# RWKV, quantised FFN and attention on one core: layernorm roots moved to a seed and a cubic, two operations moved to GpSimd, and new instruction orders

## What is computed

```python
def wkv(time_decay, time_first, k, v):
    w, u = -jnp.exp(time_decay), time_first
    def step(carry, kv):
        aa, bb, pp = carry
        ww = u + kk
        qq = jnp.maximum(pp, ww)
        e1, e2 = jnp.exp(pp - qq), jnp.exp(ww - qq)
        out = (e1 * aa + e2 * vv) / (e1 * bb + e2)
        qq2 = jnp.maximum(pp + w, kk)
        ...
for l in range(L):                        # 4 layers
    h = layernorm(x, ln1_w[l], ln1_b[l]); hh = time_shift(h)
    k, v, sr = ...                        # three products of mixes of h and hh
    x = x + (sr * wkv(...)) @ Wo[l].T
    h = layernorm(x, ln2_w[l], ln2_b[l]); hh = time_shift(h)
    x = x + sigmoid(xr @ Wcr[l].T) * (square(relu(xk @ Wck[l].T)) @ Wcv[l].T)
```

## Time and profile before

| | |
|---|---|
| time, median of 3 runs | 1373.0 us (1369.5 to 1373.78) |
| profiled execution, span on the core | 1368.5 us |
| the profiled execution's own time | no other than the span is recorded for it; the runs lie 1.0 to 5.3 us above the span |
| TensorE busy | 1303.0 us, 95% |
| VectorE busy | 1238.3 us, 90% |
| ScalarE busy | 1257.6 us, 92% |
| GpSimd busy | 1122.6 us, 82% |

### The profile page before, as it was taken

How to read it: one execution, slowest core, us unless ns; L and a number is a source line. 1 busy time by engine, 2 the same in 40 slices (tenths; PEclk the granted TensorE clock), 3 DMA queues, 4 the chain that set the end, 5 groups by cost and what they waited for, 6 DMA issues and landing times.

```text
span 1368.5 us, 23485 instructions
## 1 busy us (share of the span) xinstructions
PE 1303.0 (95%) x7285; PEld 935.9 (68%) x7285; DVE 1238.3 (90%) x2169; ACT 1257.6 (92%) x2539; POOL 1122.6 (82%) x1216
## 2 busy tenths in 40 slices
PE   3799999999999999999999999988999998899997
PEld 1356677667766677667766677766777876677776
DVE  6999999999999999999999999569999577978994
ACT  6899999999999999999999999877887899998884
POOL 6888998888888888888899999979998465666784
PEclk9899999999999999999999999999999999999999
DMA  7000000000000000000000000010000000000011
GB/s 237 1 1 1 1 1 1 1 21 13 1 0 2 1 1 1 1 1 1 1 1 1 8 24 21 27 32 1 1 1 1 2 1 1 1 16 16 24 32 39
DMA packets 26923, 18.54 MB, mean 14 GB/s; under 512 B 1072, under 2 KB 26160, under 8 KB 26800
## 3 DMA queue, kind: packets, MB, share of 16 engines
q1 hardware_dynamic: 26800, 17.05, 4.2%
HBM read 12.85 MB, written 4.19 MB: 12 GB/s over the span
## 4 chain that ended last, share of the span: by engine, by line
PE 67%; ACT 11%; DVE 9%; POOL 6%; issue 5%; DMA 0%; SPq 0%; DVEq 0%; ACTq 0%; POOLq 0%
PE ps L1154 12%; PE ps L1137 12%; PE ps L1213 5%; PE ps L1037 4%; PE ps L1192 4%; PE ps L1185 4%; PE ps L1144 3%; PE ps L1124 3%; PE ps L1089 3%; PE ps L1090 3%; PE ps L1102 3%; PE ps L1082 3%; PE ps L1263 3%; PE ps L1201 2%; PE ps L1245 2%
## 5 line engine op out<-in xcount | busy, mean ns | idle before, releaser
L1137 PE MATMUL ps<-xk,W 128*128 128x512 f32 x512 | 250.7, 593 | 1.4 <-ACT kf L864 1.4
L1154 PE MATMUL ps<-W,kf 128*128 128x128 f32 x2048 | 249.6, 275 | 0.0
L754 ACT ACTIVATE z<-X,ln_rs 128x128 f32<-128x128 f32 x512 | 239.7, 720 | 3.7 <-POOL ln_rs L603 3.7
L1154 PEld LDWEIGHTS ps<-W,kf 128*128 128x128 f32 x2048 | 239.2, 192 | 2.3 <-issue 1.0
L864 ACT ACTIVATE kf<-ps 128x512 f32<-128x512 f32 x256 | 186.6, 817 | 0.5 <-PE ps L1137 0.5
L871 ACT ACTIVATE kf<-kf 128x1024 f32<-128x1024 f32 x128 | 164.6, 1286 | 0.0
L1037 PEld LDWEIGHTS ps<-idn,z 128*128 128x128 f32 x664 | 83.1, 143 | 113.3 <-issue 87.3
L1137 PEld LDWEIGHTS ps<-xk,W 128*128 128x128 f32 x512 | 91.9, 190 | 92.1 <-issue 89.0
L710 POOL TENSOR_TENSOR W<-W,hsc 128x704 f32<-128x704 f32 x64 | 88.8, 1388 | 59.0 <-DVE W L493 58.8
L1037 PE MATMUL ps<-idn,z 128*128 128x128 f32 x664 | 102.0, 277 | 29.8 <-ACT z L754 20.7
L601 POOL TENSOR_TENSOR ln_rs<-ln_rs,mhalf 128x8 f32<-128x8 f32 (+1 forms) x70 | 127.9, 1827 | 0.0
(11 more groups left out here) (176 smaller groups left out, 3962.5 us busy)
## 6 DMA issues: line engine op xcount, KB each, us to landing
X<-x_in SPq DMA_DIRECT2D x16, 256.0 KB, 6.9
xi<-x_in SPq DMA_DIRECT2D x16, 256.0 KB, 2.9
out<-X SPq DMA_DIRECT2D x16, 256.0 KB, 2.3
W<-weights SPq DMA_DIRECT2D x4, 832.0 KB, 8.4
W<-fp4w SPq DMA_DIRECT2D x1, 560.0 KB, 3.8
row<-rows SPq DMA_DIRECT2D x1, 192.0 KB, 2.9
wqkv<-qkv SPq DMA_DIRECT2D x1, 96.0 KB, 5.7
idn<-ident SPq DMA_DIRECT2D x1, 64.0 KB, 3.1
```

Of the source, the lines that this page charges most:

```text
L754: last = e.activation(chunk(dst, j), chunk(src, j), ACT.Identity, bias=rs[:, 1, j:j + 1], scale=rs[:, 0, j:j + 1])
L1137: e.matmul((pF0, pF1)[f % 2][:, :], w_of(r, WCK + f), xk[r % 2][:, :], start=True, stop=True).then_inc(kf_mm[f], 1)
L1154: last = e.matmul(chunk(pKV, j), kf[r % 3][:, f, j * 128:(j + 1) * 128], w_of(r, WCV + f), start=f == 0 and j == 0, stop=f == 3, skip_grou ...
```

## The change

What it does:

- The root of both RWKV norms leaves GpSimd. VectorE computes v (`root_v`), ScalarE takes a seed from the bits of v (`root_seed`, an exponential of the integer reading), and VectorE refines it by a cubic in six steps (`root_a`, `root_h`, `root_t`, `root_w`, `root_y`, `root_m`), the last of which is minus mean times root. All work on 4 or 8 columns.
- `norm1` goes from ScalarE to GpSimd, as four tensor_scalar instructions.
- `arg_r` goes from VectorE to GpSimd, as min(d, 30 - time_first); time_first is now the bias of `exp_r`.
- `init_affine` signals in one semaphore instead of two.
- The call lists of all four engines are in another order with other offsets; they begin at tick -1 and end ten ticks sooner.

```diff
 CUBIC, LEAD = 0.9991106956842978, 1.000889996847986
-CAP = 30.0
+CAP, BIG = 30.0, 3.0e38
+ROOT_SEED = LN2 * 63.5 - 0.18117945103602753
+ROOT_B, ROOT_C, ROOT_R = 1.2010822484555626, 1.4256689734683168, 1.8119322349731568
...
-TICKS = FFN2_AT + 35
+TICKS = FFN2_AT + 25
+FIRST = -1
...
+        def root_slot(s):
+
+            lo, hi = 0 if s < NR else NT, 2 * NT if s >= LN2_LAG else NT
+            return n_1.rs2[s % 3][:, :, lo:hi], n_1.st2[s % 3][:, lo:hi, :]
...
+                e.tensor_scalar(capt[:, :], vec[:, TF, :], -1.0, CAP, ALU.mult, ALU.add).then_inc(vecs_done, 1)
...
+            def root_v(s):
+                if 0 <= s < NR + LN2_LAG:
+                    rs, st = root_slot(s)
+                    w.wait_ge(n_1.stats, min(s + 1, NR))
+                    w.wait_ge(n_2.stats, s - LN2_LAG + 1)
+                    w.wait_ge(root_seeded, s - 2)
+                    e.tensor_scalar(rs[:, 2, :], st[:, :, 2], 1.0 / 128.0, EPS, ALU.mult, ALU.add).then_inc(root_v_done, 1)
+
+            def root_a(s):
+                if 0 <= s < NR + LN2_LAG:
+                    rs, _ = root_slot(s)
+                    w.wait_ge(root_seeded, s + 1)
+                    e.scalar_tensor_tensor(out=rs[:, 5, :], in0=rs[:, 2, :], scalar=-1.0, in1=rs[:, 3, :],
+                                           op0=ALU.mult, op1=ALU.mult).then_inc(*own.next())
+                    root_a_at[s] = own.so_far()
+
+            def root_h(s):
+                if 0 <= s < NR + LN2_LAG:
+                    rs, _ = root_slot(s)
+                    w.wait_ge(*root_a_at[s])
+                    e.tensor_tensor(rs[:, 4, :], rs[:, 5, :], rs[:, 3, :], ALU.mult).then_inc(*own.next())
+                    root_h_at[s] = own.so_far()
+
+            def root_t(s):
+                if 0 <= s < NR + LN2_LAG:
+                    rs, _ = root_slot(s)
+                    w.wait_ge(*root_h_at[s])
+                    e.scalar_tensor_tensor(out=rs[:, 5, :], in0=rs[:, 4, :], scalar=ROOT_B, in1=rs[:, 4, :],
+                                           op0=ALU.add, op1=ALU.mult).then_inc(*own.next())
+                    root_t_at[s] = own.so_far()
+
+            def root_w(s):
+                if 0 <= s < NR + LN2_LAG:
+                    rs, _ = root_slot(s)
+                    w.wait_ge(*root_t_at[s])
+                    e.scalar_tensor_tensor(out=rs[:, 6, :], in0=rs[:, 5, :], scalar=ROOT_C, in1=rs[:, 3, :],
+                                           op0=ALU.add, op1=ALU.mult).then_inc(*own.next())
+                    root_w_at[s] = own.so_far()
+
+            def root_y(s):
+                if 0 <= s < NR + LN2_LAG:
+                    rs, _ = root_slot(s)
+                    w.wait_ge(n_1.z, min(s - 2, NR))
+                    w.wait_ge(n_2.z, s - LN2_LAG - 2)
+                    w.wait_ge(*root_w_at[s])
+                    e.scalar_tensor_tensor(out=rs[:, 0, :], in0=rs[:, 4, :], scalar=ROOT_R, in1=rs[:, 6, :],
+                                           op0=ALU.add, op1=ALU.mult).then_inc(*own.next())
+                    root_y_at[s] = own.so_far()
+
+            def root_m(s):
+                if 0 <= s < NR + LN2_LAG:
+                    rs, st = root_slot(s)
+                    w.wait_ge(*root_y_at[s])
+                    e.scalar_tensor_tensor(out=rs[:, 1, :], in0=st[:, :, 1], scalar=-1.0, in1=rs[:, 0, :],
+                                           op0=ALU.mult, op1=ALU.mult).then_inc(n_1.nr, 1)
...
-            def arg_r(r):
-                if 0 <= r < NR:
-                    w.wait_ge(rwkv_done, r - 1)
-                    w.wait_ge(d_done, r + 1)
-                    e.tensor_scalar(er[r % 2][:, :], dd[r % 2][:, :], v_of(r, TF), CAP, ALU.add, ALU.min).then_inc(argr_done, 1)
 
...
+            def normalise(g, n, src, dst):
+                rs = g.of(g.rs, n)
+                w.wait_ge(g.nr, n + g.lag + 1)
+                for j in range(NT):
+                    last = e.tensor_scalar(chunk(dst, j), chunk(src, j), rs[:, 0, j:j + 1], rs[:, 1, j:j + 1], ALU.mult, ALU.add)
+                last.then_inc(g.z, 1)
+
+            def norm1(r):
+                if 0 <= r < NR:
+                    w.wait_ge(turned1, r - 1)
+                    normalise(n_1, r, X[r % NB], z1[r % 2])
 
...
+            def arg_r(r):
+                if 0 <= r < NR:
+                    w.wait_ge(vecs_done, VECS)
+                    w.wait_ge(rwkv_done, r - 1)
+                    w.wait_ge(d_done, r + 1)
+                    e.tensor_scalar(er[r % 2][:, :], dd[r % 2][:, :], col(capt, r), -BIG, ALU.min, ALU.max).then_inc(argr_done, 1)
...
+            def root_seed(s):
+                if 0 <= s < NR + LN2_LAG:
+                    rs, _ = root_slot(s)
+                    w.wait_ge(n_1.nr, s - 2)
+                    w.wait_ge(root_v_done, s + 1)
+                    e.activation(rs[:, 3, :], rs[:, 2, :].bitcast(I32), ACT.Exp, bias=ROOT_SEED,
+                                 scale=-LN2 / 2.0 ** 24).then_inc(root_seeded, 1)
...
             def exp_r(r):
                 if 0 <= r < NR:
                     w.wait_ge(argr_done, r + 1)
-                    e.activation(er[r % 2][:, :], er[r % 2][:, :], ACT.Exp).then_inc(er_done, 1)
+                    e.activation(er[r % 2][:, :], er[r % 2][:, :], ACT.Exp, bias=v_of(r, TF)).then_inc(er_done, 1)
 
```

The lists, at the calls the prediction speaks of (VectorE's, GpSimd's, then ScalarE's):

```diff
-            for t in range(TICKS):
+            for t in range(FIRST, TICKS):
...
+                root_h(t - 3)
...
+                root_t(t - 3)
...
+                root_w(t - 3)
+                root_v(t - 2)
...
+                root_y(t - 3)
...
+                init_affine(t - 1)
...
+                root_m(t - 3)
...
+                prepare(t)
...
+                root_a(t - 2)
...
-                arg_r(t - 5)
...
-                init_affine(t - 1)
...
-                prepare(t - 2)
...
-            for t in range(TICKS):
+            for t in range(FIRST, TICKS):
...
-                add_res(ffn_job(t + 4))
...
+                norm1(t - 5)
...
+                weights_scaled(t - Q_AT - 12)
...
+                add_res(ffn_job(t + 6))
+                arg_r(t - 7)
...
-                rsqrts(t - 4)
...
-                weights_scaled(t - Q_AT - 5)
...
-                norm1(t - 3)
...
+                root_seed(t - 1)
```

More of the change, by code:

```diff
@@ L165, in hybrid_program @@
         xi_here = [sem("xi_here0"), sem("xi_here1")]
[L166 to L168 removed]
+        consts, ew_done, vecs_done, w_mixed, we_done = [sem(k) for k in ("consts", "ew", "vecs", "w_mixed", "we")]
+        in_x, root_v_done, root_seeded = sem("in_x"), sem("root_v"), sem("root_seed")
         turned1, h1_done, dh1_done, xt_done, xr_done, k_done, v_mm, r_mm, sr_done = [sem(k) for k in (
@@ new lines, in scalar @@
+            for t in range(FIRST, TICKS):
+                relu(t - 10, 3)
+                keep_pt(att_job(t - 6), 1)
+                relu(t - 10, 2)
+                keep_av(att_job(t - 5))
+                keep_pt(att_job(t - 6), 2)
+                square(t - 10, 0)
+                keep_h1(t - 3)
+                exp_k(t - 5)
+                exp_d(t - 5)
+                exp_r(t - 5)
+                square_1(t - 6)
+                weights_out(t - Q_AT - 14)
+                a_exp(att_job(t - 5), 1)
+                keep_pt(att_job(t - 6), 3)
+                tanh_c(t - 10)
+                root_seed(t - 1)
+                keep_ag(att_job(t - 4))
+                norm2(t - 8)
+                a_exp(att_job(t - 5), 2)
+                keep_hq(ffn_job(t - 7), 2)
+                keep_ax(att_job(t - 3))
+                a_exp(att_job(t - 5), 3)
+                relu(t - 9, 1)
+                fx_magic(ffn_job(t - 2))
+                silu(ffn_job(t - 4), 1)
+                keep_fx(ffn_job(t - 3))
+                fh_magic(ffn_job(t - 5), 0)
+                relu(t - 9, 0)
+                silu(ffn_job(t - 4), 2)
+                silu(ffn_job(t - 4), 3)
+                square(t - 10, 1)
+                tanh_r(t - 5)
+                seeds(t - 5)
+                keep_h2(t - 8)
+                put_x(ffn_job(t - 7))
+                f_z(ffn_job(t))
+                silu(ffn_job(t - 3), 0)
+                a_z(att_job(t - 1))
+                keep_hq(ffn_job(t - 6), 0)
+                fh_magic(ffn_job(t - 5), 1)
+                init_z(t + 1)
+                keep_x(ffn_job(t - 7))
+                keep_hq(ffn_job(t - 6), 1)
+                args(t - 4)
+                keep_pt(att_job(t - 5), 0)
+                a_exp(att_job(t - 4), 0)
@@ L1315, in sync @@
+                turn1(t - 3)
+                output(t - 7)
         def sync():
```

268 lines of the change are left out of this document (104 added, 164 removed).

## The result

The changed kernel takes **1611.0 us** (median of 4 runs, 1609.6 to 1612.4) against 1371.3 us for the kernel before in the same measurement (1369.5 to 1373.8): a ratio of 1.174, 95% interval 1.172 to 1.176. It is slower by 240 us. The forecast was 1374, the range 1362 to 1386.

The account below looks back on a forecast made before the run. TensorE was taken to bound the steady state at 13.10 us a tick, unchanged, and VectorE the fill. 1373.0 + 3.7 (fill) - 2.5 (transition) = 1374.2 us, with a range for 8 in 10 of 1362 to 1386.

Parts of the forecast that it names:

- The first affine: Sign in the fill: VectorE's first affine starts near 13 us, not at 10.04, after the weight work.
- the first key product: Sign in the fill: TensorE's first key product moves from 22.04 to about 28.5 us.
- the start: Late start of the fill: only VectorE's added idle time counts, 7.8 against 7.3 us, so +0.5 us.
- The step that failed: VectorE in the steady state: seven small root instructions at 0.09 us, 0.63 in all; tick 12.9 us, still covered.
- 0.2 us of cover: Steady state: room left between VectorE's forecast tick of 12.9 us and TensorE's 13.10.
- The second failed step: GpSimd in the steady state: loses 3.2 us of roots, gains 2.7 of scalings and cap; tick 10.9 us, covered.
- Rival 2: Steady state and fill: VectorE becomes the bound at 0.17 us per small root step, tick 13.4, 1398 us; chance 0.10.
- Rival 4: Steady state: GpSimd too slow, new work costing 5.5 us, tick 13.7, 1406 us; chance 0.03.
- The transition: Passage to the quantised FFN: add_res two ticks earlier takes two of its runs out of GpSimd's rounds, -2.5 us.
- the 12 us of unknown on either side: Rest of the FFN and attention blocks: new places taken as 0 change, with 12 us either way as ends.
- Rival 1: Behind 890 us: new orders close 12 of TensorE's 31.4 us of idle time, 1364.7 us; chance 0.30.

Follow-up runs that it names:

- experiment 4: Changed kernel, same instructions reordered: VectorE's mixes and root steps in one stretch, GpSimd's norm1 directly behind sub_dh1; 1547.6 us.
- experiment 1: Kernel before plus one independent 8-column VectorE probe before the pp scan: two SBUF inputs 1397.5 us, tensor_scalar with one 1397.8, SBUF and PSUM 1371.6.
- experiment 8: Kernel before with only add_res moved two ticks earlier; 1371.3 us, ratio 0.9996.

## Why the prediction was wrong

**What held.** The prices, one by one: GpSimd's scaling 0.45 us (forecast 0.40); undisturbed small steps 0.08 to 0.11 us start to start, with `root_v` at 0.21 (0.09); VectorE's tick less its stalls 13.05 us (12.9). The cap has 1.04 us, but starts while `xc` runs; clear of such work it is 0.68 us in experiment 4 (forecast 1.06). The first affine at 12.79 us (13.2); the first key product at 30.77 (28.5), so the start cost more than the +0.5 put on it: 8.7 us of lag at the first scan, of which 5.2 come with the new orders alone (31.02 in the run with the old division of work, 25.79 in the kernel before). TensorE was idle for 48.5 of the first 107 us, not 37.

**The step that failed** is VectorE's: "Start to start is what the engine pays when the next instruction doesn't need the result, and in the new order other work stands between most of the steps." The 0.09 us came from one instruction with a single input. Beside GpSimd a step of 8 columns takes up to 2.1 us. In the tick shown three of the seven steps (`a`, `h`, `w`) and two of the four mixes (`xt`, `sr`), which I had not touched because the diff only moved them, cost 3.3 us, and in the ticks of 17.5 us `a` costs 1.2 more. With 0.2 us of cover that is the whole loss of the steady state: TensorE, bound at 13.10, waits for VectorE at 16.3 to 17.5.

**The second failed step** is GpSimd's: "A tick is then 11.4 - 3.2 + 2.7 = 10.9 us: covered." The sum was right as work (10.6 in experiment 4). But the 3.2 us taken out were the stretch beside which VectorE ran its mixes undisturbed, and the 2.7 us put in are work that shuts it out. GpSimd's 10.6 us and VectorE's 3.4 have to fit into a tick one behind the other: 14.0 us, worked out from experiment 4. Rival 2 named the right engine, and its 1398 came from a fixed cost of 0.17 us; the mechanism was another. Rival 4 had GpSimd too slow, and it wasn't.

**It was in the trace.** A GpSimd instruction on 8 columns in the kernel before, in two RWKV ticks. In the first the mix `xt` started at 507.83, ahead of it, in the second at 678.97, behind it:

```profile
508.12 0.56 POOL L599 TENSOR_SCALAR ln_rs<-ln_st 128x8 f32<-128x8 f32 x1
...
678.93 0.24 POOL L599 TENSOR_SCALAR ln_rs<-ln_st 128x8 f32<-128x8 f32 x1
```

The same work, 0.56 and 0.24 us. Its last step has 0.45 there. And the old order put all four mixes and the cap exactly over the GpSimd roots, for which I found no reason in their data.
The Trainium skill ("SBUF — State Buffer", section "SBUF: two separate sides") states it outright: one pair of SBUF ports is shared by VectorE and GpSimd as an exclusive lock, taken by a VectorE instruction in a two-port mode or with two SBUF inputs. The runs agree for GpSimd's 512-column products (beside one the probe took 0.94 us with two SBUF inputs and 0.14 with one in PSUM), and the tensor_scalar of experiment 1 fits its two-port mode, which no run shows by itself. By this rule the moved steps and mixes could meet GpSimd's work, and it was no rival of mine.
They do not agree with its "for the whole instruction": the power of 1.9 us held nothing up.

**The transition** was to give 2.5 us: not there alone (experiment 8). From the last scan to the end the changed kernel takes 532.9 us against 523.2, 9.8 more, inside the 12 us of unknown on either side. Rival 1 did not come.
